# One instruction list for all engines, or a list for each: a two-layer attention and FP4 network on one core

## The chip, the cores and the metric

The kernel runs on one core of one Trainium2 chip. The metric is the time on the device in microseconds (us). The kernel before takes 1997.37 us, the median of three runs (1996.66 to 2009.59).

Five engines work side by side, and each runs its own instructions in the order in which they stand: TensorE (PE: matmuls and transposes into PSUM), VectorE (DVE), ScalarE (ACT: functions from tables, and copies), GpSimd (POOL: elementwise work on SBUF) and SyncE (SP: it starts the transfers). They meet at semaphores: an instruction that waits holds up everything behind it on its own engine.

## The reference

The input has 32 batches of 256 tokens of 128 numbers; every batch goes through two layers.

```python
xn = layernorm(x)
# layer 0: cosine attention (16 heads of 8), plus softmax attention and a top-2 of 8 mixture
cos = clip(l2norm(Q) @ l2norm(K).T, -0.999, 0.999)
W   = (1 - arccos(cos) / pi) ** 16             # normalised over a row
x   = x + (W @ V) @ Wo + bo + softmax(q @ k.T / sqrt(8)) @ v + moe(xn)
xn = layernorm(x)
# layer 1: one causal head, and a gated network whose operands are rounded to FP4 in blocks of 16
x  = x + causal_attention(xn) + fp4_linear(silu(fp4_linear(xn, gate)) * fp4_linear(xn, up), down)
```

## The kernel before

The weights are loaded, rounded and transposed once (the first 42 us). Then the work of a batch is cut into some hundred small **stages**, named by a word and a number: `("quantx", 7)` is the eighth of the nine roundings of the second layer's input. A stage may have instructions on several engines: `("c", 3)` is four matmuls on PE and the clip of their result on DVE.

What sets the order is a table written out by hand, `SCHEDULE` (lines 54 to 78). Each entry is a stage, its number and a lag. The program runs in steps t; in each step every engine walks through the table (`steps`, line 389) and issues those instructions of a stage that are its own, for batch t + lag. So one step holds work of four batches (lags 1, 0, -1 and -2), and in the middle of the run each step finishes one batch. The loop holds two steps, since buffers are chosen by the batch's parity. Here all engines read the same table, so that the stages stand in the same order on each of them.

The stages that the prediction speaks of, by their lines:

- `c`, `m`, `e` (PE lines 1055, 1064, 1082 and 1084): the score matmuls, eight units each per batch. They share two PSUM slots in turn: a unit can start when the unit two places before it has been read, by DVE (`c` at line 866, `m` at 872) or by ACT (`e`, an Exp into `prob`).
- The cosine curve, four pairs per batch, each 128 x 2048: `sq` (POOL, line 511), `ln` and `sigm` (ACT, in `root`), `mul` (`curve` times `root`: pairs 0 and 2 on POOL, line 514; 1 and 3 on DVE, line 862), `arctan`, `wln` and `wexp` (ACT, in `curve`). `pvw` is the matmul with V (PE, line 1208).
- `quantx` 0 to 8 (DVE, lines 417 to 433): the FP4 rounding of the second layer's input. Its result is transposed by PE (`xqT`, line 1169) and copied by ACT (`xqT`). `quanth` is the same for the hidden layer.
- `proj` (line 1024): PE writes Q, K and V of a half of the tokens into two banks; ACT reads one, DVE the other (line 783).
- `experts` 0 and 1: for each token half PE writes four experts into a bank (lines 1031 and 1032), and DVE adds them up, token halves in turn (line 846). `choose` 0 to 5 (DVE) works out the gate; `choose` 3 is line 826, `choose` 4 lines 830 and 831.
- `finc`, `ocT`, `wo`, `ln1`, `rstd1`, `xn1T`: the output of the cosine attention, its projection (DVE reads it at line 913), and the second layernorm, whose square root goes over ACT (Ln and Exp, `ln1`) and comes back to DVE (line 755, `rstd1`).
- `norm`, `guess`, `newton`, `unit`, `high`, `stack`, `stackT`: Q and K are normalised and split into two halves of 16 bits each. `unit` (line 530) and `stack` (line 547) are POOL's, `high` 2 and 3 ACT's; `stackT` is transposed by PE (line 1043) and copied by DVE (line 858).
- `table` 0 and 1 (ACT, lines 590 and 658): the two loads of function tables in a step. Table 1 holds Sigmoid and Arctan, table 0 Ln and Exp; all Ln and Exp of a step lie between table 0 and table 1.

The other PSUM use goes through two banks (`MISC`, lines 82 to 84) in turn, in the order of the table, so that here too a use waits until the use two places before it has been read (`bank_read`, line 349).

Of the kernel before, what the change touches and what calls it, by code (L numbers as in the profile page):

```python
# [52 lines left out]

SCHEDULE = [
    ("table", 0, -1), ("c", 2, 0), ("s1", 0, -2), ("wln", 0, -1), ("fadd", 0, -1), ("finf", 0, -1), ("wln", 1, -1),
    ("quanth", 1, -2), ("wexp", 0, -1), ("s1e", 0, -2), ("c", 3, 0), ("wexp", 1, -1), ("wln", 2, -1), ("wexp", 2, -1),
    ("c", 4, 0), ("quanth", 2, -2), ("experts", 0, 0), ("wln", 3, -1), ("c", 5, 0), ("pvw", 0, -1), ("quanth", 3, -2),
    ("ln0", 0, 1), ("c", 6, 0), ("experts", 1, 0), ("sq", 2, 0), ("wexp", 3, -1), ("pvw", 1, -1), ("pvw", 2, -1),
    ("quanth", 4, -2), ("rstd0", 0, 1), ("p1T", 0, -2), ("ln", 0, 0), ("quanth", 5, -2), ("pvw", 3, -1),
    ("xnT", 0, 1), ("maxT", 0, 0), ("quanth", 6, -2), ("quanth", 7, -2), ("c", 7, 0), ("ln", 1, 0), ("proj", 0, 1),  # L60
    ("oC", 0, -1), ("e", 0, 0), ("proj", 1, 1), ("e", 1, 0), ("gmax", 0, 1), ("quanth", 8, -2), ("ln", 2, 0),
    ("finc", 0, -1), ("o1", 0, -2), ("sq", 3, 0), ("norm", 0, 1), ("ocT", 0, -1), ("gexp", 0, 1), ("e", 2, 0),
    ("e", 3, 0), ("wo", 0, -1), ("guess", 0, 1), ("ln1", 0, -1), ("pvf", 0, 0), ("e", 4, 0), ("rstd1", 0, -1),
    ("e", 5, 0), ("pvf", 1, 0), ("ln", 3, 0), ("choose", 0, 1), ("xn1T", 0, -1), ("high", 0, 1), ("high", 1, 1),
    ("e", 6, 0), ("quantx", 0, -1), ("stack", 0, 1), ("newton", 0, 1), ("quantx", 1, -1), ("high", 2, 1), ("e", 7, 0),
    ("quantx", 2, -1), ("stack", 1, 1), ("choose", 1, 1), ("quantx", 3, -1), ("quantx", 4, -1), ("stackT", 0, 1),
    ("quantx", 5, -1), ("unit", 0, 1), ("quantx", 6, -1), ("stackT", 1, 1), ("pvf", 2, 0), ("choose", 2, 1),
    ("load", 0, 1), ("stack", 2, 1), ("quantx", 7, -1), ("stack", 3, 1), ("m", 0, 1), ("residual", 0, 1),
    ("high", 3, 1), ("m", 1, 1), ("quantx", 8, -1), ("table", 1, 0), ("p1", 0, -1), ("choose", 3, 1), ("m", 2, 1),
    ("stackT", 2, 1), ("pvf", 3, 0), ("sigm", 0, 0), ("stackT", 3, 1), ("m", 3, 1), ("sigm", 1, 0), ("mul", 0, 0),  # L70
    ("xqT", 0, -1), ("m", 4, 1), ("sigm", 2, 0), ("hT", 0, -2), ("hT", 1, -2), ("arctan", 0, 0), ("mul", 1, 0),
    ("c", 0, 1), ("hmul", 0, -1), ("gu", 0, -1), ("mul", 2, 0), ("m", 5, 1), ("sq", 0, 1), ("sq", 1, 1), ("m", 6, 1),
    ("mul", 3, 0), ("sigm", 3, 0), ("oF", 0, 0), ("arctan", 1, 0), ("hmul", 1, -1), ("choose", 4, 1), ("gu", 1, -1),
    ("arctan", 2, 0), ("quanth", 0, -1), ("c", 1, 1), ("choose", 5, 1), ("m", 7, 1), ("down", 0, -2),
    ("arctan", 3, 0),
]
# [1158 lines left out]
```

## Time and profile before

| | |
|---|---|
| median of 3 runs | 1997.37 us |
| span of the profiled execution (the only time given for it) | 2001.0 us |
| DVE busy | 1799.0 us, 90% of the span |
| ACT busy | 1773.5 us, 89% |
| PE busy | 1475.5 us, 74% |
| POOL busy | 1189.6 us, 59% |
| DMA | 11.19 MB, 6 GB/s in the mean |
| table loads on ACT, lines 590 and 658 | 32 and 32 |

The span is 3.6 us over the median, 0.2%. A step can be told by the load of table 0 (line 590), which stands once in each. A busy share says how long an engine had an instruction in work, and an instruction that waits for a port of the memory counts as work too.

### The profile page before, as it was taken

To read this page: it belongs to the slowest core of one execution; us is meant where nothing else is said; L and a number is where in the kernel's file an instruction comes from. 1 tells how busy PE (TensorE), PEld (TensorE's weight loads), DVE (VectorE), ACT (ScalarE), POOL (GpSimd) and SP (SyncE) were. 2 spreads that over 40 slices of the span, in tenths; PEclk is the share of its full clock that TensorE was granted. 3 is DMA by queue.
4 is the path that set the end of the run, shared out by engine and by line. 5 is a ranking of instruction groups with operands and counts; after the bars stand their busy time and mean duration, and the time that the engine had idled before them with its cause. 6 is when DMAs were issued, how large, how long until landed. Compare 5 with 4: busy or idle time off the path is not lost.

```text
span 2001.0 us, 38650 instructions
## 1 busy us (share of the span) xinstructions
PE 1475.5 (74%) x12022; PEld 748.7 (37%) x12022; DVE 1799.0 (90%) x4073; ACT 1773.5 (89%) x1888; POOL 1189.6 (59%) x547
## 2 busy tenths in 40 slices
PE   2677777777777777787777777687777768777765
PEld 1223333433343433344334333343333434333433
...
GB/s 41 4 3 1 6 1 5 6 6 6 6 5 0 6 6 6 6 6 3 3 6 5 6 6 6 0 6 6 5 6 6 6 0 6 6 5 6 4 4 6
DMA packets 21058, 11.19 MB, mean 6 GB/s; under 512 B 1431, under 2 KB 20953, under 8 KB 20956
## 3 DMA queue, kind: packets, MB, share of 16 engines
...
## 4 chain that ended last, share of the span: by engine, by line
ACT 40%; DVE 21%; issue 21%; PE 15%; DVEq 1%; ACTq 1%; SPq 0%; DMA 0%; POOL 0%
ACT curve L559 23%; ACT root L559 7%; PE psM L1024 3%; PE psM L1177 3%; DVE nmax L872 3%; ACT prob L559 2%; ACT L590 2%; PE psV L1208 2%; DVE h L433 1%; DVE stkT L858 1%; ACT p L559 1%; PE psS L1082 1%; DVE xqT L427 1%; DVE curve L862 1%; DVE oh L826 1%
## 5 line engine op out<-in xcount | busy, mean ns | idle before, releaser
L511 POOL TENSOR_TENSOR root<-curve 128x2048 f32<-128x2048 f32 x128 | 478.9, 3742 | 452.4 <-DVE curve L866 452.4
L559 ACT ACTIVATE curve<-curve 128x2048 f32<-128x2048 f32 x384 | 716.1, 1906 | 4.5 <-POOL curve L514 2.3
L559 ACT ACTIVATE root<-root 128x2048 f32<-128x2048 f32 x256 | 484.5, 1906 | 0.0
L514 POOL TENSOR_TENSOR curve<-curve,root 128x2048 f32<-128x2048 f32 x64 | 353.7, 5539 | 109.5 <-ACT root L559 109.5
L866 DVE TENSOR_SCALAR curve<-psS 128x1024 f32<-128x1024 f32 x256 | 308.0, 1214 | 1.9 <-PE psS L1055 1.9
L872 DVE TENSOR_REDUCE nmax<-psS 128x4 f32<-128x1024 f32 x256 | 302.9, 1214 | 2.4 <-PE psS L1064 2.4
L559 ACT ACTIVATE prob<-psS 128x1024 f32<-128x1024 f32 x256 | 257.0, 1031 | 24.2 <-PE psS L1084 22.2
L547 POOL TENSOR_TENSOR stk<-qk,stk 128x512 f16<-128x512 f32 x128 | 151.2, 1192 | 67.7 <-ACT stk L559 67.3
L1064 PE MATMUL psS<-stkT 32*128 32x256 f16 x1024 | 107.2, 307 | 87.5 <-DVE stkT L858 39.5
L1208 PE MATMUL psV<-curve,vc 128*32 128x256 f32 x2048 | 142.2, 410 | 35.1 <-ACT curve L559 31.4
L862 DVE TENSOR_TENSOR curve<-curve,root 128x2048 f32<-128x2048 f32 x64 | 156.9, 2452 | 6.1 <-ACT root L559 6.1
L1032 PE MATMUL psM<-we,xnT 128*128 128x512 f32 x256 | 158.1, 703 | 0.0
L1208 PE MATMUL psV<-prob,vf 128*32 128x256 f32 x2048 | 155.0, 426 | 0.6 <-ACT prob L559 0.6
L1177 PE MATMUL psM<-wguT,xqT 128*128 128x352 f32 x256 | 127.3, 635 | 32.8 <-ACT hqT L559 26.1
L846 DVE SCALAR_TENSOR_TENSOR acc<-psM,comb,acc 128x128 f32<-128x128 f32 x512 | 135.3, 337 | 7.9 <-PE psM L1032 7.9
L1194 PE MATMUL psM<-wdT,hqT 128*128 128x128 f32 (+1 forms) x384 | 84.8, 402 | 66.1 <-DVE h L964 65.4
L1055 PE MATMUL psS<-stkT 32*128 32x256 f16 x1024 | 109.6, 319 | 30.1 <-DVE curve L866 15.7
L1043 PE MATMUL psM<-ident,stk 128*128 128x128 f16 x1024 | 87.2, 234 | 33.2 <-ACT xn1T L559 26.0
L1194 PEld LDWEIGHTS psM<-wdT,hqT 128*128 128x128 f32 (+1 forms) x384 | 75.5, 298 | 77.8 <-DVE h L964 76.7
L1208 PEld LDWEIGHTS psV<-curve,vc 128*32 128x32 f32 x2048 | 62.6, 116 | 111.1 <-issue 78.3
L1082 PE MATMUL psS<-stkT 32*128 32x256 f16 x1024 | 98.6, 283 | 4.1 <-ACT prob L559 2.5
L1084 PE MATMUL psS<-mT,pickb 32*128 32x256 bf16 x1024 | 97.3, 280 | 0.0
...
## 6 DMA issues: line engine op xcount, KB each, us to landing
...
```

Source lines behind the costliest of these rows:

```text
L511: nc.gpsimd.tensor_tensor(root[:, two], curve[:, p, two], curve[:, p, two], ALU.mult).then_inc(s_sq, 1)
L514: nc.gpsimd.tensor_tensor(curve[:, p, two], curve[:, p, two], root[:, two], ALU.mult).then_inc(s_half[0], 1)
L547: nc.gpsimd.tensor_tensor(lo, src, hi, ALU.subtract).then_inc(s_stk, 1)
L559: return nc.scalar.activation(out, in_, func, **kw)
L846: nc.vector.scalar_tensor_tensor(acc[:, p, j, :], bank[:, (e % 4) * D:(e % 4 + 1) * D], comb[:, p, j, e:e + 1], acc[:, p, j, :], ALU.mult, ...
L862: nc.vector.tensor_tensor(curve[:, p, two], curve[:, p, two], root[:, two], ALU.mult).then_inc(s_half[1], 1)
L866: nc.vector.tensor_scalar(curve[:, p, arg * UC:(arg + 1) * UC], psS[:, slot_of(stage, arg), :, :, :].rearrange("p a k q -> p (a k q)"), CO ...
L872: nc.vector.tensor_reduce(nmax[:, :, 2 * arg:2 * arg + 2].rearrange("p j a -> p a j"), psS[:, slot_of(stage, arg), :, :, :], AX.X, ALU.max ...
L1032: mm(bank[:, :], xnT[:, j * P:(j + 1) * P], we[:, 4 * arg:4 * arg + 4, :].rearrange("p e f -> p (e f)"), start=False, stop=True).then_inc( ...
L1177: ins = mm(bank[:, 0:I], xqT[:, arg * P:(arg + 1) * P], wguT[:, m, :], start=True, stop=True)
L1194: ins = mm(bank[:, j * D:(j + 1) * D], hqT[0:CH[c], j, c, :], wdT[0:CH[c], c, :], start=(c == 0), stop=(c == NCH - 1))
L1208: ins = mm(psV[rows(hh), kind, half, :], head_window(v, p, kt, head_at(g, hh)), w[:, hh, kt, :], start=(g % 2 == 0 and kt == 0), stop=(g % ...
```

## The change

`SCHEDULE` becomes `ORDER`, with a list for each engine. The stages and the instructions in them are the same, with the same semaphores; their places differ, and some have another lag on an engine. The two rings of PSUM (`SCORES` and `MISC`) now follow PE's list. ACT still loads two tables in a step.

```diff
-SCHEDULE = [
-    ("table", 0, -1), ("c", 2, 0), ("s1", 0, -2), ("wln", 0, -1), ("fadd", 0, -1), ("finf", 0, -1), ("wln", 1, -1),
...
-LAG = {(s, a): lag for s, a, lag in SCHEDULE}
+ORDER = {
+    "sync": [
+        ("load", 0, 1), ("down", 0, -2),
+    ],
+    "tensor": [
+        ("c", 4, 0), ("c", 5, 0), ("c", 6, 0), ("experts", 0, 0), ("c", 7, 0), ("e", 0, 0), ("experts", 1, 0),
...
+MOST_LAG = max(-lag for order in ORDER.values() for s, a, lag in order)
+LAG = {(s, a): lag for s, a, lag in ORDER["tensor"]}
...
-MISC = [(s, a, use) for s, a, lag in SCHEDULE for use in range(USES.get(s, 0))]
...
+MISC = [(s, a, use) for s, a, lag in ORDER["tensor"] for use in range(USES.get(s, 0))]
...
-        def steps(eng, run):
+        def steps(eng, order, run):
...
-                for stage, arg, lag in SCHEDULE:
+                for stage, arg, lag in order:
...
-            steps(sp, run)
+            steps(sp, ORDER["sync"], run)
```

Three places show it. The line numbers of the changed kernel are 22 higher.

**ACT, from `ln1` to the first `sigm`.** `lnv` and `rstd` are `ln1` here, `prob` is an `e`, `root` is `ln` before the table load and `sigm` behind it, `stk` is a `high`. Before:

```order
L559 ACTIVATE rstd1<-lnv1 128x2
...
L559 ACTIVATE prob<-psS 128x1024
...
L559 ACTIVATE root<-root 128x2048
L559 ACTIVATE xn1T<-psM1 128x256
...
L559 ACTIVATE stk<-qk 128x64x8
L658 ACT_TABLE_LOAD
L559 ACTIVATE u1T<-psM0 128x256
L559 ACTIVATE root<-root 128x2048 x2
L559 ACTIVATE xqT<-psM0 128x256
```

In the change:

```order
L581 ACTIVATE rstd1<-lnv1 128x2
L581 ACTIVATE lnn<-n2 128x64
L581 ACTIVATE rn<-lnn 128x64
...
L581 ACTIVATE prob<-psS 128x1024
L581 ACTIVATE root<-root 128x2048
...
L581 ACTIVATE stk<-qk 128x64x8
L680 ACT_TABLE_LOAD
L581 ACTIVATE root<-root 128x2048
L581 ACTIVATE xqT<-psM0 128x256
L581 ACTIVATE xn1T<-psM1 128x256
L581 ACTIVATE root<-root 128x2048
```

Between `ln1` and the first `sigm` one `e` (of four before), `xn1T` and `u1T` (the copy of `p1`) are gone and `guess` has come; `xqT` stands behind the first `sigm` and no longer behind the second.

**DVE, the end of the rounding `quantx` and `choose` 3.** `xq1` and `xqT` are `quantx`, `oh` is `choose` 3 where it is made from `iota8`, `nmax` is an `m`. Before:

```order
L431 SCALAR_TENSOR_TENSOR xq1<-xqT,xq1 128x256
...
L872 TENSOR_REDUCE nmax<-psS 128x2x2
...
L433 TENSOR_TENSOR xq1<-xq1,qxa 128x256
L930 COPY v1<-psM1 128x2x128
...
L826 TENSOR_TENSOR oh<-iota8,topf 128x16 x2
```

In the change:

```order
L848 TENSOR_TENSOR oh<-iota8,topf 128x16 x2
...
L451 SCALAR_TENSOR_TENSOR xq1<-xqT,xq1 128x256
...
L453 SCALAR_TENSOR_TENSOR xq1<-xqT,xq1 128x256
...
L455 TENSOR_TENSOR xq1<-xq1,qxa 128x256
...
L852 TENSOR_TENSOR oh<-oh 128x16
L853 TENSOR_TENSOR ge<-ge,gs 128x16
```

`choose` 3 now stands ahead of the last three roundings; between these stands one `m` each, and `choose` 4 stands right behind the last. Ahead of all this DVE has the same stages since `rstd1` in both kernels.

**PE, the start of a step.** `ber` and `we` are `experts`, `curve,vc` is a `pvw`, `mT` is an `e`, the rest with `stkT` is `c`. Before:

```order
L1055 MATMUL psS<-stkT 128x256 x4
L1031 MATMUL psM0<-ber,onesb 128x512
L1032 MATMUL psM0<-we,xnT 128x512
...
L1055 MATMUL psS<-stkT 128x256 x4
...
L1208 MATMUL psV<-curve,vc 32x256 x8
...
L1055 MATMUL psS<-stkT 128x256 x4
...
L1031 MATMUL psM0<-ber,onesb 128x512
```

In the change:

```order
L1077 MATMUL psS<-stkT 128x256 x4
...
L1053 MATMUL psM0<-ber,onesb 128x512
...
L1077 MATMUL psS<-stkT 128x256 x4
...
L1104 MATMUL psS<-stkT 128x256
L1106 MATMUL psS<-mT,pickb 128x256
...
L1053 MATMUL psM0<-ber,onesb 128x512
L1054 MATMUL psM0<-we,xnT 128x512
```

`e` 0 now stands between the last `c` and the second half of the experts, and the first half stands behind `c` 6 instead of `c` 4. On DVE `c` 4 is now the last stage of a step, and the next step goes `c` 5, `ln0`, `experts` 0, `c` 6, `c` 7, `experts` 1.

## Rows read from the trace of the kernel before

**Rows 1.** Windows, two steps: length, busy us of PE, PEld, DVE, ACT, POOL; clock.

```profile
1003.46:1066.26 62.80, 45.76 (x372) 23.45 (x373) 58.96 (x126) 54.97 (x58) 37.07 (x16) 0.85 0.02 5
...
1181.78:1239.03 57.25, 44.73 (x382) 22.13 (x380) 53.89 (x126) 54.98 (x58) 36.92 (x16) 0.92 0.02 5
```

**Rows 2.** Timeline of ACT: start, length, line; the load of table 0.

```profile
181.40 1.28 ACT L590 ACT_TABLE_LOAD   x1
...
1831.10 1.28 ACT L590 ACT_TABLE_LOAD   x1
```

**Rows 3.** Waits of DVE: total us, times, longest.

```profile
DVE qk L783 <- PE psM L1024: 59.6, 37, 4.3
```

**Rows 4.** Timelines of POOL, DVE and ACT in the step from 1003.46.

```profile
1045.47 4.58 POOL L514 TENSOR_TENSOR curve<-curve,root 128x2048 f32<-128x2048 f32 x1 [2.24 <-ACT root L559]
...
1045.50 4.58 DVE L826 TENSOR_TENSOR oh<-iota,topf 128x16 f32<-128x16 f32 x2
...
1052.66 0.38 ACT L559 ACTIVATE xqT<-psM 128x256 f32<-128x256 f32 x1 [5.47 <-PE psM L1169]
```

**Rows 5.** Two lines of DVE: shortest, median and longest in ns.

```profile
L826 DVE TENSOR_TENSOR oh<-iota,topf x64: 156/160/4497, 60.7 to 1876.1; 128x16 f32<-128x16 f32 x64
...
L419 DVE TENSOR_SCALAR qxa<-qxa x32: 166/171/948, 157.2 to 1973.2; 128x16 f32<-128x16 f32 x32
```

**Rows 6.** Timeline of ACT in the step from 1003.46.

```profile
1033.18 0.26 ACT L559 ACTIVATE lnn<-n 128x64 f32<-128x64 f32 x1
...
1033.85 0.20 ACT L559 ACTIVATE rstd<-lnv 128x2 f32<-128x2 f32 x1
1034.00 1.94 ACT L559 ACTIVATE prob<-psS 128x1024 f32<-128x1024 f32 x2
1035.82 1.91 ACT L559 ACTIVATE root<-root 128x2048 f32<-128x2048 f32 x1
...
1038.79 0.65 ACT L559 ACTIVATE stk<-qk 128x512 f16<-128x512 f32 x1
...
1040.89 1.28 ACT L658 ACT_TABLE_LOAD   x1
```

**Rows 7.** Timeline of DVE in two steps: start of `rstd1`, `quantx` 8.

```profile
1034.09 0.32 DVE L755 SCALAR_TENSOR_TENSOR lnt<-mv,rstd 128x2 f32<-128x2 f32 x1 [0.71 <-ACT rstd L559]
...
1044.83 0.41 DVE L433 TENSOR_TENSOR xq<-xq,qxa 128x256 f32<-128x256 f32 x1
...
1096.80 0.32 DVE L755 SCALAR_TENSOR_TENSOR lnt<-mv,rstd 128x2 f32<-128x2 f32 x1 [0.74 <-ACT rstd L559]
...
1106.63 0.41 DVE L433 TENSOR_TENSOR xq<-xq,qxa 128x256 f32<-128x256 f32 x1
```

**Rows 8.** Timelines of POOL and DVE in the step from 1066.26: `mul`.

```profile
1107.93 11.07 POOL L514 TENSOR_TENSOR curve<-curve,root 128x2048 f32<-128x2048 f32 x2 [1.66 <-ACT root L559]
...
1112.05 2.56 DVE L862 TENSOR_TENSOR curve<-curve,root 128x2048 f32<-128x2048 f32 x1
```

**Rows 9.** Timelines of PE and DVE near 1130: `experts`, `ln0` and `c`.

```profile
1127.63 0.38 PE L1031 MATMUL psM<-ber,onesb 3*128 3x512 bf16 x1
...
1130.38 0.39 PE L1055 MATMUL psS<-stkT 32*128 32x256 f16 x4
...
1131.55 2.06 DVE L846 SCALAR_TENSOR_TENSOR acc<-psM,comb,acc 128x128 f32<-128x128 f32 x8
...
1135.45 0.48 DVE L745 BATCH_NORM_STATS2 st<-xt 128x6 f32<-128x128 f32 x2
...
1136.16 1.23 DVE L866 TENSOR_SCALAR curve<-psS 128x1024 f32<-128x1024 f32 x1
```

**Rows 10.** Timeline of DVE in the step from 1003.46: `finc` to `wo`.

```profile
1027.78 0.17 DVE L798 TENSOR_REDUCE gm<-gl 128x2 f32<-128x16 f32 x1
...
1029.78 0.42 DVE L899 TENSOR_TENSOR oc<-psM,rsC 128x256 f32<-128x256 f32 x1
...
1032.15 0.42 DVE L913 TENSOR_TENSOR x<-psM,acc 128x256 f32<-128x256 f32 x1
```

More of the change, by code:

```diff
@@ L48 @@
 HIGH_ON_POOL = (0, 1)
-SCHEDULE = [
-    ("table", 0, -1), ("c", 2, 0), ("s1", 0, -2), ("wln", 0, -1), ("fadd", 0, -1), ("finf", 0, -1), ("wln", 1, -1),
[L56 to L76, printed above, removed]
@@ L77 @@
-LAG = {(s, a): lag for s, a, lag in SCHEDULE}
+ORDER = {
[4 more added lines that the diff above has]
+        ("c", 4, 0), ("c", 5, 0), ("c", 6, 0), ("experts", 0, 0), ("c", 7, 0), ("e", 0, 0), ("experts", 1, 0),
+        ("pvw", 0, -1), ("pvw", 1, -1), ("p1T", 0, -2), ("pvw", 2, -1), ("e", 1, 0), ("o1", 0, -2), ("xnT", 0, 1),
+        ("pvw", 3, -1), ("e", 2, 0), ("proj", 0, 1), ("proj", 1, 1), ("finc", 0, -1), ("pvf", 0, 0), ("e", 3, 0),
[5 rows of a table added]
+        ("maxT", 0, 1),
+    ],
+    "vector": [
+        ("c", 5, 0), ("ln0", 0, 1), ("experts", 0, 0), ("c", 6, 0), ("c", 7, 0), ("experts", 1, 0), ("quanth", 0, -2),
+        ("rstd0", 0, 1), ("quanth", 1, -2), ("quanth", 2, -2), ("xnT", 0, 1), ("quanth", 3, -2), ("o1", 0, -2),
+        ("quanth", 4, -2), ("quanth", 5, -2), ("quanth", 6, -2), ("quanth", 7, -2), ("proj", 0, 1), ("quanth", 8, -2),
+        ("proj", 1, 1), ("finc", 0, -1), ("gmax", 0, 1), ("norm", 0, 1), ("wo", 0, -1), ("ln1", 0, -1),
+        ("rstd1", 0, -1), ("choose", 0, 1), ("xn1T", 0, -1), ("choose", 1, 1), ("quantx", 0, -1), ("newton", 0, 1),
+        ("quantx", 1, -1), ("stackT", 0, 1), ("stackT", 1, 1), ("quantx", 2, -1), ("choose", 2, 1), ("quantx", 3, -1),
+        ("quantx", 4, -1), ("quantx", 5, -1), ("choose", 3, 1), ("quantx", 6, -1), ("m", 0, 1), ("quantx", 7, -1),
+        ("m", 1, 1), ("quantx", 8, -1), ("choose", 4, 1), ("m", 2, 1), ("m", 3, 1), ("stackT", 2, 1), ("m", 4, 1),
+        ("p1", 0, -1), ("stackT", 3, 1), ("mul", 1, 0), ("m", 5, 1), ("m", 6, 1), ("m", 7, 1), ("hmul", 0, -1),
+        ("mul", 3, 0), ("c", 0, 1), ("maxT", 0, 1), ("hmul", 1, -1), ("c", 1, 1), ("choose", 5, 1), ("c", 2, 1),
+        ("down", 0, -2), ("c", 3, 1), ("finf", 0, 0), ("s1", 0, -1), ("c", 4, 1),
+    ],
+    "scalar": [
+        ("wln", 0, -1), ("wln", 1, -1), ("wexp", 0, -1), ("wln", 2, -1), ("maxT", 0, 0), ("wexp", 1, -1),
[4 rows of a table added]
+        ("high", 3, 1), ("table", 1, 0), ("sigm", 0, 0), ("xqT", 0, -1), ("xn1T", 0, -1), ("sigm", 1, 0),
+        ("p1", 0, -1), ("sigm", 2, 0), ("oF", 0, 0), ("hT", 1, -2), ("sigm", 3, 0), ("arctan", 0, 0), ("gu", 0, -1),
+        ("arctan", 1, 0), ("arctan", 2, 0), ("gu", 1, -1), ("arctan", 3, 0), ("table", 0, 0),
+    ],
+    "gpsimd": [
+        ("sq", 1, 0), ("fadd", 0, -1), ("sq", 2, 0), ("sq", 3, 0), ("norm", 0, 1), ("high", 0, 1), ("high", 1, 1),
+        ("stack", 0, 1), ("stack", 1, 1), ("unit", 0, 1), ("stack", 2, 1), ("stack", 3, 1), ("mul", 0, 0),
+        ("mul", 2, 0), ("residual", 0, 1), ("sq", 0, 1),
+    ],
+}
@@ L86 @@
+SCORES = [(s, a, 0) for s, a, lag in ORDER["tensor"] if s in ("c", "m", "e")]
 assert len(SCORES) % 2 == 0
@@ L399, in steps @@
                     step(i * 2 + (2 + k), k)
-            for t in range(B - 2, B - min(LAG.values())):
+            for t in range(B - 2, B + MOST_LAG):
                 step(t, t % 2)
@@ L551, in run @@
                     nc.gpsimd.tensor_tensor(acc[:, p, :, :], acc[:, p, :, :], of[:, :, :], ALU.add).then_inc(s_acc2, 1)
-            steps(pool, run)
+            steps(pool, ORDER["gpsimd"], run)
         @block.scalar
@@ L712, in run @@
                     activate(hqT[:, j, :, :].rearrange("p c q -> p (c q)"), bank[:, 0:NCH * P], ACT.Copy).then_inc(s_hT, 1)
-            steps(act, run)
+            steps(act, ORDER["scalar"], run)
         @block.vector
@@ L980, in run @@
                                             x2[:, :, :], ALU.add).then_inc(s_y, 1)
-            steps(dve, run)
+            steps(dve, ORDER["vector"], run)
         @block.tensor
@@ L1211, in pv @@
                 ins.then_inc(done, 1)
-            steps(pe, run)
+            steps(pe, ORDER["tensor"], run)
 INPUTS = ["L0_attn_x", "L0_attn_Wq", "L0_attn_Wk", "L0_attn_Wv", "L0_attn_Wo", "L0_attn_bo", "L0_ffn_W_qkv",
```

1 line of the change is left out of this document (removed), and 9 rows, old and new, of the table ORDER.

## The prediction, made before the changed kernel ran

> **What bounds the kernel now.** I read the page first: DVE and ACT are each busy for about nine tenths of the span, PE and POOL far less, and in the chain that ended last ACT and DVE take turns. So the question is how the two are interlocked. The loads of table 0 cut the run into steps: from the one at 181.40 to the one at 1831.10 there are 28, which makes 1649.7 us or **58.92 us a step** [rows 2]. Windows between such loads give the shape: ordinary steps take 57.2 to 58 us, with DVE busy for 53.9 and ACT for 55.0, and **every fourth takes 62.8** [rows 1]. The mean of the ordinary ones is then (4 x 58.92 - 62.80) / 3 = 57.6.
>
> ACT has the same 55.0 in both kinds, DVE five more in the long one. What DVE does there stands in the third view: its two tiny `choose` 3 instructions, 0.16 us each as a rule, take 4.58 together, from 1045.50 to 1050.08, and `mul` 0 on POOL runs from 1045.47 to 1050.05 [rows 4, 5]. DVE got there 0.03 us after POOL had begun, and waited for the whole of POOL's instruction; ACT then sat idle for 5.47 at `xqT`, behind DVE's next stages [rows 4]. The Trainium skill has a rule for it (page "SBUF — State Buffer", section "Who interferes with whom"): a DVE instruction with two SBUF inputs and a GpSimd instruction that reads SBUF exclude each other, and the holder keeps the port for its whole length. The trace agrees, with 4.50 against 0.16. I call this **a strike**.
>
> In an ordinary step DVE is nearly saturated: its 57.6 are 53.9 of work, 1.6 at the second `proj` (59.6 us in all, some 1.6 a time) [rows 3], 0.7 at `rstd1`, which waits for ACT [rows 7], and some 1.4 of small gaps. ACT's 55.0 are the floor that a better order can reach.
>
> **The change, part by part.** No instruction is added or removed, table loads included; only places and waits change. DVE's ledger of one step, from the ordinary 57.6:
>
> 1. *`proj`.* `quanth` 8, 0.9 of work, now stands between the two halves, and ACT is asked for less in between. The wait of 1.6 [rows 3] falls by between 0.9 and 1.5: **-1.2**.
>
> 2. *`finc` to `wo`.* The result has to go DVE, PE (`ocT`), ACT, PE (`wo`) and back, 1.95 from the end of `oc` at 1030.20 to `wo` at 1032.15 [rows 10]. Before, `o1` and `norm` filled it; now `gmax` and `norm` do, and `o1` was worth 0.75. The wait is between 0 and 0.75: **+0.3**. `ln1` to `rstd1` keeps its 0.7.
>
> 3. *`experts`.* Each half of a stage takes PE (1130.38 - 1127.63) / 2 = 1.37 [rows 9]. Now `c` 6 must follow DVE's `c` 4 (they share a slot), which is the last stage of DVE's step, and both halves of `experts` 0 stand behind `c` 6: 0.35 + 2 x 1.37 + 0.15 for semaphores = 3.25 after `c` 4 ends. DVE meanwhile has `c` 5 (1.15), `ln0` (0.71) and one addition (0.26) [rows 9], so it waits 1.15. `experts` 0 ends at 3.25 + 1.8 = 5.05, `c` 6 at 6.25. Only then can `e` 0 start on PE, since it takes `c` 6's slot, and `experts` 1 stands behind `e` 0, for which I take 0.5: at 6.8, with halves at 8.2 and 9.6. DVE would want them at 7.4; its last seven additions end at 11.4 instead of 9.4. In all 1.15 + 2.0 = **+3.1**. Bounds: 0, if PE gets ahead in a way that I don't see, and 3.5; I take 3.0, as all of it comes from rows.
>
> 4. *Small stretches by the same port.* DVE's short two-input instructions are held up for up to 0.8 us by POOL's `unit` and `stack` (line 419: 0.17 or 0.95, every second step [rows 5]). The copies `stackT` now lie where `unit` and `stack` run. Between 0 and -1.5: **-0.7**.
>
> Sum: 57.6 - 1.2 + 0.3 + 3.0 - 0.7 = **59.0 without any strike**.
>
> 5. *Strikes.* How long after `ln1` does POOL start `mul` 0, and how long does DVE need from `rstd1` (which starts 0.04 after `ln1` on ACT) to the end of `quantx`? Before, `mul` 0 came 1045.47 - 1034.05 = 11.4 after `ln1`; DVE's last rounding ended 1045.24 - 1034.09 = 11.15 after `rstd1` in one step and 1107.04 - 1096.80 = 10.24 in the next, always just ahead of `mul` 0 [rows 4, 6, 7]. Now ACT's path is shorter: `guess` 0.5, one `e` 0.97, `ln` 1.9, two `e` 1.94, two `high` 1.3, the table 1.28, `sigm` 1.9 = **9.8, less 0.2 to 0.4 of overlap** [rows 6]. DVE has the same stages before its last rounding as before, and `choose` 3 besides. By the old 10.2 and 11.2, `quantx` 7 or 8 comes 0.5 to 1.5 after `mul` 0 has begun, and both have two SBUF inputs. They are struck. In the steps of the shorter kind (10.24) the stretches of point 4 may go, and up to 1.5 saved brings the rounding to the end just in time; in the other kind, 0.9 longer, not. A strike holds DVE for the rest of `mul` 0: 4.5 less 0.4 to 1 = **3.9** (the long step showed 4.4 on DVE, 62.80 - 57.6 = 5.2 in all). ACT, which needs the rounding at 9.3 for `xqT`, gets it at some 15 and idles 5.6; its 55.0 + 0.6 + 5.6 = 61.2 stay under DVE's 59.0 + 3.9 = 62.9.
>
> The rest moves at no cost: SP's two stages stand last in nobody's way (6 GB/s in all), POOL has 37 of 58 us of work, so its early `sq` 1 and late `residual` have cover. Start and end of the run (the first 181 and the last 170 us) keep the same chain of stages; I take 0 for them, within 5 us either way.
>
> **Forecast.** A strike in every second step: 59.0 + 3.9 / 2 = 60.95, 2.03 a step over now, x 28 = +57 us on a span of 2001.0. The median is 0.2% under this span, so 1997.4 x 2058 / 2001 = **2054 us**, 2.8% slower. Chance 0.32.
>
> **Rivals.**
> - *A strike in every step* (the old lengths of rows 7 hold in both kinds): 62.9, 28 x 4.0 = +111, **2108 us**. For it: both old lengths are over 9.6. Against: the saved stretches. 0.22.
> - *No strike, DVE's new wait at `experts` eats the gain*: 59.0, **1999 us**, no change. It decides if DVE's last rounding starts less than 9.4 after `rstd1`. 0.16.
> - *Faster: ACT becomes the bound.* No strike, and the 3.0 at `experts` overlap with waits that DVE would have had anyway; then ACT's 55.0 and some 1 us of its own waits decide, 56 to 57.5 a step: 28 x (-2.9 to -1.4) = -82 to -40, **1916 to 1957 us**. For it: the regular strike of today is gone, since `choose` 3 now comes long before `mul` 0, and that alone is worth 1.3 a step. It decides where the sum of points 2 and 3 is under 1 us. 0.20.
> - *A second strike in each step, `mul` 1 behind `mul` 2.* Since `sigm` 2 now follows `xqT` by a fixed 4.4 on ACT, POOL's `mul` 2 and DVE's `mul` 1 get ready within some 0.5 of one another, 5 to 5.5 after the last rounding. If POOL is first, DVE waits 4.2 more and ACT waits for `arctan` 1: 67.1, **2226 us**. Against it: today a DVE `mul` that waits while `mul` 0 runs gets the port before POOL's next instruction (2.56 long, while POOL's two took 11.07 together [rows 8]). By the page's words alone (the one that starts first keeps the port) nothing would give a waiting DVE its turn between two POOL instructions, and this rival would be the rule; rows 8 speak against that. 0.10.
>
> That the change does not do what it says can be left out: the lists as built differ as stated, and ACT keeps two table loads a step as before.
>
> **The numbers.** A difference of 1%, 20 us, is about what a measurement here tells from none. Faster: the fourth case, 0.20. Same: the third and the lower edge of the forecast, 0.18. Slower: the rest, 0.62. The range 1930 to 2125 takes in the first three cases and most of the fourth; it leaves out the double strike (0.10) and the best of the fourth.
>
> **What would show it.** In the profile after: DVE's wait before its additions at `experts` (line 868) near 28 x 3 in all; the wait at the second `proj` mostly gone; the longest of `choose` 3 down to 0.16, and instead `quantx` 7 or 8 (lines 453 and 455) or `choose` 4 with a longest of about 4; ACT idle at `xqT` for 5 to 6 us in such steps. I am wrong if the roundings end before `mul` 0 begins, or if PE delivers the experts in time.

## The result and the profile after

The changed kernel takes **2460.9 us** (median of four runs, 2459.8 to 2465.2), the kernel before 1998.2 (four runs): a ratio of **1.230, with a 95% interval from 1.227 to 1.234**. The forecast was 2054, in a range from 1930 to 2125. The direction was right; the loss was eight times as large.

The page of the changed kernel gives the busy times first: us, share of the span, instructions.

```profile
span 2459.5 us, 38594 instructions
...
PE 1722.0 (70%) x12022; PEld 831.8 (34%) x12022; DVE 1999.4 (81%) x4073; ACT 1784.6 (73%) x1888; POOL 1149.5 (47%) x547
...
PE 38%; DVE 34%; issue 21%; ACT 4%; DVEq 1%; POOL 1%; SPq 0%; ACTq 0%; DMA 0%; POOLq 0%
```

The instructions are the same, yet DVE is busy for 200.4 us more than before, and idle for 258.1 more; together that is the whole difference of the spans, 458.5, as it must be. PE is busy for 246.5 more and now leads the chain that ended last (the last row), where ACT and DVE took turns before. The timeline of ACT has the load of table 0 at both ends of 28 steps:

```profile
202.33 1.28 ACT L612 ACT_TABLE_LOAD   x1
...
2255.32 1.28 ACT L612 ACT_TABLE_LOAD   x1
```

A step takes (2255.32 - 202.33) / 28 = **73.32 us**, against 58.92 [rows 2]. The 28 steps take 72.7 to 74.4, and two in a row look like this: no step stands out as every fourth did before [rows 1].

```profile
1154.55:1227.90 73.35, 53.38 (x375) 25.87 (x375) 61.82 (x126) 55.45 (x58) 35.69 (x16) 0.71 0.01 4
1227.90:1301.33 73.43, 52.76 (x375) 25.66 (x375) 62.00 (x126) 55.34 (x58) 35.71 (x16) 0.73 0.01 4
```

DVE has 62 of work where it had 53.9, and ACT its usual 55. The granted clock (the third column from the end) is 0.71 to 0.73 where it was 0.85 to 0.92.

**The busy time.** The costly groups of DVE: total us, mean ns, idle us before them.

```profile
L868 DVE SCALAR_TENSOR_TENSOR acc<-psM,comb,acc 128x128 f32<-128x128 f32 x512 | 144.2, 344 | 239.5 <-PE psM L1054 239.4
...
L884 DVE TENSOR_TENSOR curve<-curve,root 128x2048 f32<-128x2048 f32 x64 | 271.9, 4248 | 0.0
L852 DVE TENSOR_TENSOR oh<-oh 128x16 f32<-128x16 f32 x32 | 134.9, 4215 | 0.0
```

`choose` 4 (line 852), 0.17 us of work, takes 4.2 in the mean, so it is struck in practically every step: +129.6. `mul` on DVE (line 884) went from 156.9 to 271.9: +115.0. `choose` 3 gives back 30.1. How it comes about stands in the timelines of DVE and POOL, in the step from 1227.90.

```profile
1266.27 0.16 DVE L777 SCALAR_TENSOR_TENSOR lnt<-mv,rstd 128x2 f32<-128x2 f32 x1 [0.70 <-ACT rstd L581]
...
1275.49 0.41 DVE L455 TENSOR_TENSOR xq<-xq,qxa 128x256 f32<-128x256 f32 x1
1275.82 4.48 DVE L852 TENSOR_TENSOR oh<-oh 128x16 f32<-128x16 f32 x1
...
1286.03 6.28 DVE L884 TENSOR_TENSOR curve<-curve,root 128x2048 f32<-128x2048 f32 x1
...
1275.55 4.72 POOL L536 TENSOR_TENSOR curve<-curve,root 128x2048 f32<-128x2048 f32 x1 [1.40 <-ACT root L581]
1285.64 4.52 POOL L536 TENSOR_TENSOR curve<-curve,root 128x2048 f32<-128x2048 f32 x1 [5.37 <-ACT root L581]
1290.12 2.77 POOL L541 TENSOR_TENSOR acc<-xt,bob 128x256 f32<-128x256 f32 x1
```

`quantx` 8 starts 0.06 us before `mul` 0 and goes through; `choose` 4, right behind it, meets `mul` 0 and is held until 1280.2. Ten us later POOL, which had been idle for 5.37, starts `mul` 2 at 1285.64, and DVE gets to `mul` 1 0.39 later: held until 1290.1, it ends at 1292.3. Then POOL's `residual` (line 541) has to wait for it in turn (2.77 us; 0.83 in the mean before). So there are **two strikes in each step**.

**The idle time.** 231.5 of the 258.1 us are DVE's wait for the experts, 239.4 now and 7.9 before; that is 239.4 / 32 = 7.5 us a step. The timelines of PE and DVE there:

```profile
1236.77 1.12 PE L1054 MATMUL psM<-we,xnT 128*128 128x512 f32 x2
...
1238.32 2.08 PE L1054 MATMUL psM<-we,xnT 128*128 128x512 f32 x2
1240.33 0.60 PE L1077 MATMUL psS<-stkT 32*128 32x256 f16 x4
...
1244.91 2.08 PE L1054 MATMUL psM<-we,xnT 128*128 128x512 f32 x2
...
1247.45 2.08 PE L1054 MATMUL psM<-we,xnT 128*128 128x512 f32 x2
...
1240.43 1.90 DVE L868 SCALAR_TENSOR_TENSOR acc<-psM,comb,acc 128x128 f32<-128x128 f32 x7 [2.13 <-PE psM L1054]
...
1247.11 0.35 DVE L868 SCALAR_TENSOR_TENSOR acc<-psM,comb,acc 128x128 f32<-128x128 f32 x1 [2.52 <-PE psM L1054]
1249.65 1.90 DVE L868 SCALAR_TENSOR_TENSOR acc<-psM,comb,acc 128x128 f32<-128x128 f32 x7 [2.19 <-PE psM L1054]
```

Only the first half has its matmuls at 1.12 us, as before. Three take 2.08, so that a half with its first matmul costs 2.6 us where [rows 9] gave 1.37. Windows of this stretch give the granted clock (third column from the end):

```profile
1233.00:1238.00 5.00, 3.47 (x20) 1.18 (x19) 4.51 (x13) 5.00 (x4) 5.00 (x4) 0.84 0.11 31
1238.00:1243.00 5.00, 2.93 (x7) 0.63 (x6) 2.87 (x9) 4.97 (x7) 3.12 (x1) 0.50 0.01 2
1243.00:1248.00 5.00, 4.48 (x13) 1.68 (x14) 1.95 (x3) 2.90 (x3) 3.32 (x1) 0.50 0.00 0
```

From 1238 on TensorE is at the lower of its two levels, 1.2 GHz and not 2.4. PE had idled for 1.35 us up to 1236.23, waiting for DVE's `c` 4, and idled again for 2.59 up to 1243.52, waiting for `c` 6.

### The profile page after: what moved, and what is told of

Its sections match the earlier page's. It is cut to its first block, busy times and chain, and to the rows that moved or that the text cites. A ratio compares the mean times of both kernels' runs of the same rounds, so it can differ in the third digit from the quotient of the medians.

```text
span 2459.5 us, 38594 instructions
## 1 busy us (share of the span) xinstructions
PE 1722.0 (70%) x12022; PEld 831.8 (34%) x12022; DVE 1999.4 (81%) x4073; ACT 1784.6 (73%) x1888; POOL 1149.5 (47%) x547
## 4 chain that ended last, share of the span: by engine, by line
PE 38%; DVE 34%; issue 21%; ACT 4%; DVEq 1%; POOL 1%; SPq 0%; ACTq 0%; DMA 0%; POOLq 0%
PE psM L1054 10%; DVE nmax L894 6%; PE psV L1230 6%; DVE curve L888 5%; DVE curve L884 4%; PE psM L1216 4%; PE psM L1046 2%; PE psM L1053 2%; DVE acc L868 2%; PE psS L1104 2%; DVE oh L852 2%; DVE xq L453 2%; PE psM L1159 1%; PE psM L1154 1%; PE psM L1122 1%
## 5 line engine op out<-in xcount | busy, mean ns | idle before, releaser
L533 POOL TENSOR_TENSOR root<-curve 128x2048 f32<-128x2048 f32 x128 | 459.4, 3600 | 446.3 <-DVE curve L888 446.3
L536 POOL TENSOR_TENSOR curve<-curve,root 128x2048 f32<-128x2048 f32 x64 | 297.3, 4647 | 230.5 <-ACT root L581 230.5
L868 DVE SCALAR_TENSOR_TENSOR acc<-psM,comb,acc 128x128 f32<-128x128 f32 x512 | 144.2, 344 | 239.5 <-PE psM L1054 239.4
L1086 PE MATMUL psS<-stkT 32*128 32x256 f16 x1024 | 120.0, 341 | 305.5 <-DVE nmax L894 304.6
L884 DVE TENSOR_TENSOR curve<-curve,root 128x2048 f32<-128x2048 f32 x64 | 271.9, 4248 | 0.0
L1054 PE MATMUL psM<-we,xnT 128*128 128x512 f32 x256 | 248.4, 1071 | 0.0
L546 POOL TENSOR_TENSOR qsq<-qk 128x512 f32<-128x512 f32 x32 | 33.3, 1039 | 404.2 <-ACT vc L581 404.2
L1104 PE MATMUL psS<-stkT 32*128 32x256 f16 x1024 | 133.6, 292 | 114.9 <-DVE curve L888 84.4
L1077 PE MATMUL psS<-stkT 32*128 32x256 f16 x1024 | 126.6, 359 | 124.7 <-DVE curve L888 88.0
L581 ACT ACTIVATE p1T<-psM 128x384 f32<-128x384 f32 x32 | 15.7, 490 | 203.1 <-PE psM L1174 203.1
L1086 PEld LDWEIGHTS psS<-stkT 32*128 32x128 f16 x1024 | 30.7, 99 | 382.0 <-DVE nmax L894 334.0
L852 DVE TENSOR_TENSOR oh<-oh 128x16 f32<-128x16 f32 x32 | 134.9, 4215 | 0.0
L1106 PE MATMUL psS<-mT,pickb 32*128 32x256 bf16 x1024 | 132.9, 290 | 0.0
```

Of the source, the lines that this page charges most:

```text
L533: nc.gpsimd.tensor_tensor(root[:, two], curve[:, p, two], curve[:, p, two], ALU.mult).then_inc(s_sq, 1)
L536: nc.gpsimd.tensor_tensor(curve[:, p, two], curve[:, p, two], root[:, two], ALU.mult).then_inc(s_half[0], 1)
L581: return nc.scalar.activation(out, in_, func, **kw)
L852: nc.vector.tensor_tensor(oh[:, 0, :, :], oh[:, 0, :, :], oh[:, 1, :, :], ALU.add).then_inc(s_gate, 1)
L868: nc.vector.scalar_tensor_tensor(acc[:, p, j, :], bank[:, (e % 4) * D:(e % 4 + 1) * D], comb[:, p, j, e:e + 1], acc[:, p, j, :], ALU.mult, ...
L884: nc.vector.tensor_tensor(curve[:, p, two], curve[:, p, two], root[:, two], ALU.mult).then_inc(s_half[1], 1)
```

## The experiments

My theory after the result: three separate causes add up, (a) the strike on `choose` 4, (b) the strike on `mul` 1, (c) the experts behind `c` 6 and `e` 0, made worse by TensorE's lower level. Against it stood that the strikes merely cover other waits, which would come out once they are gone, and that the lower clock follows from the slow step and is no cause. Each time below is a median of four to six runs; differences are taken to 2460.9, or to the kernel before, which took 1998 to 2003 beside them.

**`choose` 4 moved to just before `choose` 5** (DVE's list alone).

```diff
-        ... ("quantx", 8, -1), ("choose", 4, 1), ("m", 2, 1), ...
+        ... ("quantx", 8, -1), ("m", 2, 1), ...
-        ... ("c", 1, 1), ("choose", 5, 1), ...
+        ... ("c", 1, 1), ("choose", 4, 1), ("choose", 5, 1), ...
```

> The changed kernel with one stage moved on DVE alone: choose 4 stands just before choose 5, long after mul 0, so that POOL's mul 0 can no longer hold it up (4.48 us in every step now). If each strike costs what its row shows and the two add up: 28 x 4.2 = 118 us less, 2343 us; the wait for mul 1 behind mul 2 stays, since DVE's path to mul 1 and, through p1, ACT's path to sigm 2 both come 4.2 earlier. If DVE's freed time is lost again to the next wait (PE's m and p1, or ACT): less than 60 us, so over 2400.

Measured: 2454.9 us (1.222, 1.212 to 1.232). That looks like the other theory, until one reads the groups of DVE in this run, and then the timelines of POOL and DVE:

```profile
L857 DVE TENSOR_TENSOR comb<-ge,oh 128x16 f32<-128x16 f32 x32 | 110.8, 3462 | 3.7
```

```profile
1295.02 3.60 POOL L533 TENSOR_TENSOR root<-curve 128x2048 f32<-128x2048 f32 x1 [10.34 <-DVE curve L888]
...
1295.16 3.49 DVE L857 TENSOR_TENSOR comb<-ge,oh 128x16 f32<-128x16 f32 x1
```

`choose` 4 is free (5.3 us in all), but its two instructions delay `choose` 5, so that POOL's `sq` 0, which `c` 1 releases, gets ahead of it by 0.14 us. The strike has moved, not gone. So the run says nothing on the price, and the place had to be one where POOL has nothing ready.

**`choose` 4 moved to just before `c` 1**: the same edit, one entry earlier.

> The changed kernel with choose 4 moved on DVE alone, this time to just before c 1: POOL is idle there, since residual is over and sq 0 waits for c 1. If the strikes are what costs the time: no DVE instruction of choose is over 0.3 us, 28 x 4.2 = 118 us less, 2343 us, with mul 1 still struck. If taking it away only lets another wait grow: over 2420.

Measured: **2340.8 us** (ratio to the kernel before 1.170, 1.166 to 1.174), 120 us less, 4.3 a step as the row of the strike had it; `choose` 4 and 5 take 5.3 and 5.2 us in all, and `mul` stays struck at 4071 ns. Cause (a) is shown.

**`mul` 1 moved up on DVE.**

```diff
-        ... ("m", 4, 1), ("p1", 0, -1), ("stackT", 3, 1), ("mul", 1, 0), ("m", 5, 1), ...
+        ... ("mul", 1, 0), ("m", 4, 1), ("p1", 0, -1), ("stackT", 3, 1), ("m", 5, 1), ...
```

> The changed kernel with mul 1 moved on DVE from behind stackT 3 to just before m 4, some 2 us earlier, so that it starts before POOL's mul 2. If the second strike is worth what its row shows: mul 1 falls from 6.28 to 2.5 us, 28 x 3.8 = 106 us less, 2355 us, and choose 4 stays at 4.2 us. If POOL's mul 2 or ACT's arctan only moves the wait to another place: less than 40 us, over 2420.

Measured: 2395.8 us (1.196, 1.190 to 1.202), 65 less. The groups of DVE in this run:

```profile
L894 DVE TENSOR_REDUCE nmax<-psS 128x4 f32<-128x1024 f32 x256 | 305.5, 1215 | 65.0 <-PE psS L1086 65.0
L884 DVE TENSOR_TENSOR curve<-curve,root 128x2048 f32<-128x2048 f32 x64 | 148.8, 2325 | 5.3 <-ACT root L581 5.3
```

The strike is gone (`mul` 271.9 to 148.8), but 60 us come back as a wait for `m` (4.8 to 65.0). Neither expectation is met. The timelines show which `m` it is: `m` 6, which PE does behind `gu` 0 (2.61 us of matmuls from 1112.45; DVE then waits 2.06 for `m` 6, up to 1115.42). So half of what the strike cost had covered a wait for PE, as the rival theory has it.

**The experts ahead on PE** (PE's list alone).

```diff
-        ("c", 4, 0), ("c", 5, 0), ("c", 6, 0), ("experts", 0, 0), ("c", 7, 0), ("e", 0, 0), ("experts", 1, 0),
+        ("c", 4, 0), ("c", 5, 0), ("experts", 0, 0), ("c", 6, 0), ("c", 7, 0), ("experts", 1, 0), ("e", 0, 0),
```

> The changed kernel with PE's list alone edited: experts 0 ahead of c 6, experts 1 ahead of e 0. Both strikes stay. By order alone, with TensorE still at its lower level of 1.2 GHz there (2.6 us per half): DVE's last addition comes 2.4 us earlier in a step, 28 x 2.4 = 66 us less, 2394 us. If the place in the list is all of the 7.5 us of waiting: 28 x 6.5 = 180 us less, 2280. If the order isn't what makes DVE wait: no change, 2461.

Measured: 2352.0 us (1.176, 1.169 to 1.183), 109 less; DVE's wait for the experts falls from 239.4 to 99.2. That lies between the two sizes: in the profile `experts` 0 now runs at full clock (1.13 us), `experts` 1 still at 2.08.

**All three moves**, with `mul` 1 just behind `m` 4 this time; I thought that the place in front of `m` 4 had made the wait.

> The changed kernel with three moves together: choose 4 to just before c 1 and mul 1 to just behind m 4 on DVE, and on PE experts 0 ahead of c 6 and experts 1 ahead of e 0. If the costs add: 4.2 + 3.8 + 3.5 = 11.5 us a step less, 61.8, 28 x 11.5 = 322 us less, 2139 us. If the strikes are mostly cover for the waits of PE (as when mul 1 alone was moved, and 60 of 123 us came back as a wait for m): 2250 or more. Level with the kernel before, 1998, or below: only if nothing else in the lists costs anything.

Measured: **2116.6 us** (1.059, 1.055 to 1.063), 344 less. `choose` 4 gave 120 alone and the experts 109, which leaves 115, 4.1 a step, for `mul` 1. That is a remainder and no measurement: this place was not run alone, the other one gave 65, and the wait for `m` is 57.6 here too. So none of the three hides another, and they give 50 us more together than the 294 of the three runs; what the 50 are is not shown.

This run holds an experiment of its own, since its steps differ. Loads of table 0, and two windows around the experts (the clock is the third column from the end):

```profile
1180.65 1.28 ACT L612 ACT_TABLE_LOAD   x1
1239.37 1.28 ACT L612 ACT_TABLE_LOAD   x1
1304.02 1.28 ACT L612 ACT_TABLE_LOAD   x1
```

```profile
1190.00:1200.00 10.00, 8.60 (x84) 3.45 (x84) 9.63 (x32) 9.97 (x11) 7.63 (x3) 1.00 0.00 1
1249.00:1259.00 10.00, 8.82 (x28) 2.29 (x32) 5.83 (x18) 7.57 (x9) 7.42 (x3) 0.50 0.00 1
```

One step takes 58.72 us, the next 64.65, by the same lists. In the first the clock is 1.00 around the experts, and DVE waits 0.22 for them; in the second it is 0.50, and DVE waits 1.29 + 0.37 + 2.47 = 4.1, and 2.0 more at `o1`. All 28 steps of this run fall in line, by the clock from 10 to 20 us behind the load: 58.7 us at 1.00, 61.0 to 61.7 at 0.83, 61.7 to 62.4 at 0.66 to 0.68, 63.7 to 63.8 at 0.59, 64.6 to 64.8 at 0.50. So the two levels of the clock go with 6 us a step here. What I still lacked was a run in which the clock alone differs.

**Fillers, at three tries.** Lists as in the changed kernel, PE repeats matmuls where it would idle.

```diff
-                    for kt in range(NT):                                            # c
+                    for kt in list(range(NT)) * {5: 3, 7: 4}.get(arg, 1):
-                    for qt_ in range(NT):                                           # m
+                    for qt_ in list(range(NT)) * {7: 9}.get(arg, 1):
```

> The changed kernel, same lists, but PE repeats matmuls where it would idle: those of m 7 nine times (while DVE is in the struck mul 1), of c 5 three times and of c 7 four times, with the same results each. If the lower level of TensorE's clock is what made experts cost 7.5 instead of 3.0 us: the halves take 1.4 us again, 28 x 4 = 112 us less, 2350 us. If the granted clock does not rise, or the lateness comes from the order alone: 2461 or some us more.

Measured: 2547.3 us (1.271, 1.264 to 1.278). My edit was at fault: `m` 7 itself waits for `m` 5, so its repeats ran late and in DVE's way (the wait for `m` 103 us). The wait for the experts fell to 224.7 only. The second try repeats `m` 6 nine times, `c` 5 four times and `c` 7 eight times.

> The changed kernel, same lists, with PE repeating matmuls in its idle stretches at other places: those of m 6 nine times (DVE is in the struck mul 1 then), of c 5 four times, of c 7 eight times. If the lower level of the clock is what made experts cost 7.5 instead of 3.0 us a step: both halves of both stages take 1.4 us, DVE's wait falls from 239 to about 110 us, 2350 us in all. If the order alone makes the wait: 239 us stay, 2461 or more.

Measured: 2465.3 us (1.232, 1.228 to 1.236), wait for the experts 225.4. Windows of PE in this run:

```profile
1230.00:1235.00 5.00, 5.00 (x24) 4.19 (x24) 4.73 (x8) 4.99 (x4) 3.54 (x1) 0.50 0.09 26
1235.00:1240.00 5.00, 4.58 (x30) 2.36 (x29) 4.16 (x8) 5.00 (x4) 4.56 (x4) 0.50 0.11 31
```

PE is busy, and the clock stays at 0.50: the fillers did not raise it where the experts run (their matmuls take 1064 ns in the mean, 1071 in the changed kernel), so the run does not decide. The next try put work that is due anyway into the gaps, `pvw`.

```diff
-        ("c", 4, 0), ("c", 5, 0), ("c", 6, 0), ("experts", 0, 0), ("c", 7, 0), ("e", 0, 0), ("experts", 1, 0),
-        ("pvw", 0, -1), ("pvw", 1, -1), ("p1T", 0, -2), ...
+        ("c", 4, 0), ("c", 5, 0), ("pvw", 0, -1), ("c", 6, 0), ("experts", 0, 0), ("c", 7, 0), ("pvw", 1, -1),
+        ("e", 0, 0), ("experts", 1, 0), ("p1T", 0, -2), ...
```

> The changed kernel with PE's list alone edited, but experts left behind c 6 and e 0: pvw 0, one microsecond of work that is due anyway, stands before c 6, and pvw 1 before e 0, in the two stretches where PE sat idle for 1.35 and 2.59 us. If the lower level of the clock, which followed those idle stretches, makes the experts late: halves of 1.4 instead of 2.6 us, DVE's wait for experts falls from 239 to some 120 us, 28 x 4 = 112 us less, 2349 us. If the place behind c 6 and e 0 makes all of it: 239 us stay, and 2430 to 2461.

Measured: 2495.2 us (1.248, 1.246 to 1.250), a miss on both sides: the experts' matmuls take 866 ns in the mean and the wait for them falls to 174.7, but what stands behind is later (DVE's wait at `proj` 22.7 to 62.8, at `o1` 28.1 to 70.7, ACT's for `xnT` 82.1). Last, fillers of the experts' own form:

```diff
+                if stage == "fill":     # before c 6 (two matmuls) and before e 0 (one); c 7 runs five times
...
+                    for n in range(2 - arg):
+                        mm(bank[:, :], xnT[:, 0:P], we[:, 4 * arg:4 * arg + 4, :].rearrange("p e f -> p (e f)"), start=True, stop=True)
```

> The changed kernel, same lists, with fillers on PE in the two idle stretches around the experts: two matmuls of the experts' own form (128 rows, 512 columns, overwritten afterwards) before c 6, five times c 7, one more such matmul before e 0. If the lower level of the clock is what made the experts cost 7.5 us: halves of 1.4 instead of 2.6 us wherever the granted clock is back at 1.00, DVE's wait falls from 239 to 120 us or less, 2350 us. If the place in the list makes it: 239 us or, with the fillers in the way, more, 2461 to 2520.

Measured: **2321.8 us** (1.161, 1.158 to 1.165), 139 less than the changed kernel, *with more work on PE and all stages in the same order*. DVE's additions and PE's experts among the groups of this run, and a window around `experts` 1:

```profile
L868 DVE SCALAR_TENSOR_TENSOR acc<-psM,comb,acc 128x128 f32<-128x128 f32 x512 | 144.2, 344 | 120.1 <-PE psM L1060 120.1
...
L1060 PE MATMUL psM<-we,xnT 128*128 128x512 f32 x256 | 145.6, 651 | 0.0
```

```profile
1179.00:1184.00 5.00, 4.94 (x46) 2.03 (x46) 3.05 (x10) 3.11 (x5) 3.60 (x1) 1.00 0.00 0
```

The experts' matmuls take 651 ns in the mean (1071 in the changed kernel, 703 before), the clock is 1.00 at `experts` 1, and the wait is halved, as expected by the theory of the clock. Both strikes are still there (4250 and 4215 ns). So of the wait of 7.5 us a step at most 3.75 is due to the order at full clock (the fillers ahead of `c` 6 and `e` 0 are in it), and as much again went with the lower level. The Trainium skill (page "TensorE: Matmul & The Clock Gate", section "HAM oscillation — how this bites in real kernels") tells of a matmul kernel that pays for the slow clock again at each burst, because PE waits in between; this run agrees (0.50 at `experts` 1 with the gaps, 1.00 with the gaps filled), and no run here shows why the busy PE of the second try stayed slow.

**The mended lists without gaps around the experts**: the three moves, and

```diff
-        ... ("c", 7, 0), ("experts", 1, 0), ("e", 0, 0), ("pvw", 0, -1), ...
+        ... ("c", 7, 0), ("pvw", 0, -1), ("experts", 1, 0), ("e", 0, 0), ...
-        ... ("wexp", 0, -1), ("wln", 2, -1), ("maxT", 0, 0), ...
+        ... ("wexp", 0, -1), ("maxT", 0, 0), ("wln", 2, -1), ...
```

> The three moves together (2116.6 us) with two more, so that PE has no gaps around the experts: pvw 0 stands before experts 1, and ACT copies maxT right behind wexp 0, one curve instruction earlier, which frees the bank for the second half of experts 0. In the three moves' run the same step took 58.7 us with the clock at 1.00 around the experts and 64.7 with it at 0.50. If the clock is what parts them, all steps come near 58.7: 28 x 3.1 = 87 us less, 2030 us. If not: 2100 or more.

Measured: **2011.8 us** (1.006, 1.004 to 1.008). The experts' matmuls take 675 ns, DVE waits for them 19.0 us in all, and most steps take 58.1 to 59.1. With six entries in other places 449 of the 460 us are back.

**Two tries to go on from there.** First, `p1` ahead of `m` 4 on PE and `xqT` behind `sigm` 1 on ACT.

> The same with two moves more: p1 ahead of m 4 on PE, and on ACT xqT behind sigm 1 instead of before it, so that ACT doesn't wait for xqT (1.2 us a step) and less for p1 (1.1 us). If ACT's waits set the end by then: 28 x 1.5 = 42 us less than without these two, about 1990. If DVE's waits set it: no gain, or a loss where mul 2 gets ahead of mul 1 again (4 us a step, 2140).

Measured: 2197.3 us (1.099, 1.097 to 1.101). The timelines of DVE and POOL:

```profile
1143.99 6.00 DVE L884 TENSOR_TENSOR curve<-curve,root 128x2048 f32<-128x2048 f32 x1
...
1143.35 4.49 POOL L536 TENSOR_TENSOR curve<-curve,root 128x2048 f32<-128x2048 f32 x1 [1.13 <-ACT root L581]
```

`sigm` 2 comes earlier, `m` 4 later, and `mul` 2 gets ahead of `mul` 1 again. It cost 185 us against the version without these two, more than one strike (28 x 4 = 112): `p1`'s copy is queued behind the struck `mul` 1 on DVE, and ACT waits 233 us for `hT`, which PE does after that. Second, the version of 2011.8 with `mul` 1 ahead of `m` 4, `m` 6 ahead of `hT` 1, and ACT's `xqT`, `sigm` 2 and `hT` 1 moved:

> The version of 2011.8 us without gaps on PE, with five moves more: on ACT xqT behind sigm 1, sigm 2 ahead of p1, hT 1 behind sigm 3 (its waits of 1.2 + 1.1 + 0.7 us a step fall to 1.3); on DVE mul 1 just before m 4, so that it waits for mul 0 and gets the port ahead of mul 2; on PE m 6 ahead of hT 1 (0.8 us of waiting on DVE). If ACT and DVE are both near their bound: 0.3 to 0.7 us a step less, 1990 to 2003. If ACT alone was the bound: 28 x 1.7 = 48 less, 1964. If mul 1 is struck again: 28 x 4 more, 2120.

Measured: 2035.6 us (1.020, 1.015 to 1.025), slower by 24. DVE's `mul` 1 does get the port ahead of `mul` 2, but it waits for it (2902 ns in the mean against 2349), and ACT's saved waits turn up at `hT` (80.4 us, 35.5 without the moves).

**The kernel before, one stage moved.** Its own strike, every fourth step on `choose` 3, was the first thing to try for a gain. `choose` 3 to before `quantx` 7:

> The kernel before with one stage moved: choose 3 stands before quantx 7, well ahead of mul 0. If the strike of every fourth step is choose 3's alone: no step of 62.8 is left, 28 x 1.3 = 36 us less, 1962 us. If the next DVE instruction with two SBUF inputs (quantx 8, mul 1) is struck in its place, or ACT bounds the step anyway: 1990 to 2000.

Measured: 2055.6 us (1.030, 1.025 to 1.034), slower. `choose` 3 now delays `quantx` 8, which had been 0.2 us ahead of `mul` 0, and that is struck instead, some eleven times: (59.9 - 13.8) / 4.3, with 13.8 in the next run, where it goes free.

```profile
L433 DVE TENSOR_TENSOR xq<-xq,qxa 128x256 f32<-128x256 f32 x32 | 59.9, 1872 | 0.1
```

`choose` 3 the other way, to just before `choose` 4:

> The kernel before with choose 3 moved the other way, to just before choose 4, where POOL is idle; quantx 8 then keeps its 0.2 us ahead of mul 0. If the strike of every fourth step goes and none takes its place: 28 x 1.3 = 36 us less, 1962 us. If another instruction is struck as often (mul 1, or quantx 8 since nothing slows the steps): 2000 or more.

Measured: **1977.6 us** (ratio 0.989, 0.987 to 0.990), the fastest of all, faster than both kernels. No strike is left. The gain is two thirds of the expected one; some of the shorter holds by `unit` and `stack` grow (DVE's `choose` 2, line 822, takes 551 ns in the mean, 404 before). `choose` 4 right behind `choose` 3, where the changed kernel is struck:

> The kernel before with choose 4 moved to just behind choose 3, 0.3 us after quantx 8, as it stands in the changed kernel; nothing else is changed. If a strike costs in this kernel what the row of the long step shows (5.2 us in all) and now comes in every step: 21 steps more of them, 21 x 5.2 = 109 us more, 2109 us. If each strike delays ACT so that the next step escapes: about 2050. If choose 4 escapes: 2000.

Measured: 2037.2 us (1.021, 1.017 to 1.025). The mean of `choose` 3 is 701 ns and of `choose` 4 440; that is some 8 and 2 strikes in 32 steps, where the kernel before has 7 and the changed kernel 30. No two struck steps follow each other here, as if a strike delayed ACT at `xqT` and with it the next `mul` 0; but with `choose` 3 early (the run of 2055.6) three steps in a row were struck, so this stays an argument. Three strikes more, at some 6 us a step, are half of the 36 us lost; the rest is open. Last, the version of 1977.6 with `quanth` 8 between the halves of `proj`, the one good idea of the change by my reckoning:

> The kernel before with choose 3 just before choose 4 (1977.6 us alone) and quanth 8 between the two halves of proj, as the changed kernel has it. If DVE's wait of 1.6 us at the second proj was on the path: 28 x 1.2 = 34 us less, 1944. If ACT's own chain sets the step by now: 1970 to 1980. If the earlier roundings or mul 1 meet POOL elsewhere: over 1980.

Measured: 2028.9 us (1.014, 1.013 to 1.016). The wait at `proj` does fall, 51.9 to 15.5, and yet the run takes 51 us more than without this move. Group of DVE, and a step of DVE and POOL:

```profile
L433 DVE TENSOR_TENSOR h<-h,qa 128x704 f32<-128x704 f32 x32 | 110.7, 3460 | 0.1
```

```profile
1041.77 3.90 DVE L433 TENSOR_TENSOR h<-h,qa 128x704 f32<-128x704 f32 x1
...
1041.32 3.60 POOL L511 TENSOR_TENSOR root<-curve 128x2048 f32<-128x2048 f32 x1 [6.19 <-DVE curve L866]
```

`quanth` 8 itself, 879 ns without a strike, has moved behind the start of a `sq` on POOL: +82.6 us. Less the 36.4 saved at `proj` that is 46, near the 51 lost, so the shorter wait may have counted; the strike outweighs it. This is the fourth time that a moved stage was struck in its new place, or pushed another one there.

## Why the prediction was wrong, point by point

- *What bounds the kernel, and the base of 57.6*: DVE was the right place to look for the strikes. But that its busy and idle time add up to the whole difference proves nothing, as they always do, and in the changed kernel PE leads the chain that ended last (38%, DVE 34%), which the prediction did not foresee.
- *Step 1, `proj`, -1.2*: right. The wait went from 59.6 [rows 3] to 22.7, -1.15 a step. In the last run above a new strike outweighed the same gain.
- *Step 2, `finc` to `wo`, +0.3*: the wait is 25.4 us in all and was 4.9, +0.64, within its bounds.
- *Step 3, the experts, +3.0 with a bound of 3.5*: **the step that failed most.** It measured 7.2. The way of the wait was right, behind `c` 6 and `e` 0; its size came from halves of 1.37 us [rows 9], measured at a granted clock of 1.00; at 0.50 a half took 2.6. With the clock kept up the wait is at most 3.75, near the estimate and a little over its bound. The windows of before show clocks of 0.85 and 0.92 [rows 1], and I took TensorE's durations there as fixed; that the new waits would leave PE idle, and the clock low after that, was in no case.
- *Step 4, the small stretches, -0.7*: right in size. DVE's busy time without the strikes and the experts' additions (+8.9) fell by 23.0, which is -0.7 a step. That is a balance: `quantx` 7, which now meets POOL's `stack`, takes 21.6 more, the rest 44.6 less. The reason given was partly wrong, since line 419 is no two-input instruction: it reads one tensor, as do lines 427, 795 and 822, which fell by 9 to 12 us each.
- *Step 5, the strike by `mul` 0*: the price (3.9) was about right, 4.3 measured by taking it away. The count was wrong: 30 of 32 steps and not every second. I took the two kinds of step of [rows 7] over, and the changed kernel has one kind only. And the condition for no strike, that the last rounding starts less than 9.4 after `rstd1`, left out what stands behind it (`choose` 4 is named only among the signs): `quantx` 8 started 9.22 after `rstd1` and escaped, and `choose` 4 was struck in its stead. ACT's 5 to 6 us of idling at `xqT` did not come (1.20 in the step shown), since the rounding was through by then.
- *The rival "a second strike, `mul` 1 behind `mul` 2", 0.10*: it happened in practically every step. The argument against it, that a waiting DVE gets the port ahead of POOL's next instruction [rows 8], holds here too (`residual` had to wait for `mul` 1) but does not apply: POOL was idle when `sigm` 2 released it. I had `mul` 2 hang on `xqT`; in fact `sigm` 2 waits for `p1`, 4.25 us of idling on ACT in this step, and so does DVE's `stackT` 3, right ahead of `mul` 1. So `mul` 2 and `mul` 1 come due within 0.4 us of each other, both by way of PE. The rule of the Trainium skill (page "SBUF — State Buffer", section "Who interferes with whom") that issue order decides was the better guide here.
- *The rivals as a set*: I gave each a chance as if only one could come, and the range stopped at 2125. A strike in every step, the second strike and a cost above the bound in step 3 came together: 59.0 + 4.3 for `choose` 4 + 4.1 for `mul` 1 + 4.2 (7.2 instead of 3.0) = 71.6 of 73.3. The 4.1 is the remainder from the three moves; by the run that moved `mul` 1 alone it would be 2.3.

What stays open: why the clock stayed low in one run with a busy PE, what the strike on `mul` 1 costs by itself, and how much of the 185 us lost by `p1` ahead of `m` 4 goes beyond the strike itself; ACT's wait for `hT` is a part that the trace shows.
